# Centering of adapter 1's tiles: from VectorE to ScalarE, with a product on GpSimd

## The reference, cut to what matters

```python
h = gelu(einsum('bsh,bhk->bsk', x, W_down[role]) + b_down[role])
y = x + einsum('bsk,bkh->bsh', h, W_up[role]) + b_up[role]
mean, var = y.mean(-1), y.var(-1)
out = (y - mean) * rsqrt(var + 1e-5) * gamma[role] + beta[role]
```

## Time and profile before

| | us |
|---|---|
| median of 3 runs | 196.28 (194.84 to 196.86) |
| profiled execution, its own time | 194.28 |
| its span, first to last instruction | 192.5 |
| TensorE, VectorE, ScalarE, GpSimd busy | 183.5, 114.7, 81.1, 42.1 |

### The profile page before, as it was taken

How to read it: one execution, slowest core, us unless ns; L and a number is a source line. 1 busy time by engine, 2 the same in 40 slices (tenths; PEclk the granted TensorE clock), 3 DMA queues, 4 the chain that set the end, 5 groups by cost and what they waited for, 6 DMA issues and landing times.

```text
span 192.5 us, 3157 instructions
## 1 busy us (share of the span) xinstructions
PE 183.5 (95%) x1031; PEld 158.0 (82%) x1031; DVE 114.7 (60%) x283; ACT 81.1 (42%) x164; POOL 42.1 (22%) x72
## 2 busy tenths in 40 slices
PE   7989999999999999999999999999999999999980
PEld 7857887979888888888888888888888989999850
DVE  2987998799658898450392622041442146558983
ACT  0643774643798206970144543003545333221340
POOL 8475667100000006000230000000110013226431
PEclk9999999999999999999999999999999999999998
DMA  3778589994301172000000070000100004432122
GB/s 103 237 218 278 166 263 262 275 306 152 109 3 60 51 239 88 0 3 0 0 0 3 0 218 0 0 0 5 55 0 0 3 0 116 125 118 78 33 61 77
DMA packets 18874, 17.83 MB, mean 93 GB/s; under 512 B 2145, under 2 KB 17322, under 8 KB 18858
## 3 DMA queue, kind: packets, MB, share of 16 engines
q1 hardware_dynamic: 17008, 14.79, 24.8%
q0 software_dynamic: 928, 2.11, 4.1%
q10 hardware_dynamic: 922, 0.73, 1.2%
HBM read 16.58 MB, written 1.05 MB: 92 GB/s over the span
## 4 chain that ended last, share of the span: by engine, by line
PE 82%; DVE 8%; DMA 4%; issue 2%; POOL 1%; ACT 0%; ACTq 0%; DVEq 0%
PE bank L640 21%; PE bank L641 20%; PE bank L642 20%; PE bank L752 5%; PE bank L768 5%; DMA stage<-in_L_cond_Wq 2%; PE bank L745 2%; PE bank L821 2%; DMA x_tok<-in_x,from_row_i 2%; PE bank L808 2%; PE bank L778 1%; DVE yA L1331 1%; PE bank L747 1%; DVE yB L1350 1%; DVE yB L1357 1%
## 5 line engine op out<-in xcount | busy, mean ns | idle before, releaser
L1412 DVE TENSOR_TENSOR g_l<-g_full,g_h 128x512 fp32r<-128x512 f32 x32 | 22.1, 692 | 38.9 <-ACT g_h L1037 38.8
L1034 ACT ACTIVATE g_full<-bank,vecs 128x512 f32<-128x512 f32 x32 | 22.1, 691 | 40.8 <-PE bank L642 39.8
L1524 POOL TENSOR_TENSOR mvA<-mvA,power 128x1 f32<-128x1 f32 x16 | 9.4, 588 | 70.2 <-DVE mvA L1267 70.1
L1037 ACT ACTIVATE g_h<-bank,vecs 128x512 fp32r<-128x512 f32 x32 | 21.9, 684 | 0.0
L1551 POOL TENSOR_TENSOR x1T<-x1T,cms_full 128x512 f32<-128x512 f32 x4 | 6.0, 1498 | 56.4 <-DVE cms_full L1427 56.4
L640 PE MATMUL bank<-g_h,mw_h 128*128 128x256 f32 (+1 forms) x48 | 16.0, 334 | 0.0
L642 PE MATMUL bank<-g_h,mw_l 128*128 128x256 f32 (+1 forms) x48 | 15.3, 318 | 0.0
L641 PE MATMUL bank<-g_l,mw_h 128*128 128x256 f32 (+1 forms) x48 | 15.3, 318 | 0.0
L640 PE MATMUL bank<-ao_h,mw_h 128*128 128x512 f32 x32 | 13.1, 411 | 0.0
L640 PE MATMUL bank<-ao_h,cw_h 128*128 128x512 f32 x32 | 12.5, 392 | 0.0
L642 PE MATMUL bank<-ao_h,mw_l 128*128 128x512 f32 x32 | 12.5, 391 | 0.0
(11 more groups left out here) (265 smaller groups left out, 441.8 us busy)
## 6 DMA issues: line engine op xcount, KB each, us to landing
stage<-in_L_cond_mW SPq DMA_DIRECT2D x6, 512.0 KB, 3.2
stage<-in_L_cond_cW SPq DMA_DIRECT2D x4, 512.0 KB, 6.7
wdA<-in_L_cond_W_down SPq DMA_DIRECT2D x14, 128.0 KB, 3.3
wuA<-in_L_cond_W_up SPq DMA_DIRECT2D x14, 128.0 KB, 3.3
wdB<-in_L_cond_W_down SPq DMA_DIRECT2D x12, 128.0 KB, 3.1
wuB<-in_L_cond_W_up SPq DMA_DIRECT2D x12, 128.0 KB, 3.0
wd_last<-in_L_cond_W_down SPq DMA_DIRECT2D x4, 128.0 KB, 2.2
wu_last<-in_L_cond_W_up SPq DMA_DIRECT2D x4, 128.0 KB, 2.1
```

The lines of the kernel that those rows point to most:

```text
L1034: act.activation(g_full[n % 2][:, 0:width], bank[b][:, 0:width], ACT.Gelu, bias=bias)
L1037: act.activation(g[0][:, j, 0:width], bank[b][:, 0:width], ACT.Gelu, bias=bias).then_inc(g_high, 1)
L1412: dve.tensor_tensor(g[1][:, j, 0:width], g_full[n % 2][:, 0:width], g[0][:, j, 0:width].bitcast(F32), ALU.subtract).then_inc(g_ready, 1)
L1524: pool.tensor_tensor(mv[:, k, 2:3], mv[:, k, 1:2], power[:, :], ALU.pow).then_inc(done, 1)
```

## The change

VectorE's centering of adapter 1 is left out. ScalarE gets a step center: it waits for rstdA_ready and computes Identity(scale * y + bias) in one activation, with the power (mvA column 2) as scale and column 3 as bias. GpSimd writes that column, -mean * power, in a tensor_scalar behind the power; link makes it wait for the power through GpSimd's own semaphore, and rstdA_ready is now raised by the product. ScalarE's new step stands where center stands in the list. Adapter 2's centering stays as it was.

```diff
--- before.py
+++ after.py
@@ -270,7 +270,7 @@
         hB = [place(f"hB{i}", [P, 2, P], F32) for i in range(XSLOTS)]
         yB = [place(f"yB{i}", [P, D], F32) for i in range(YSLOTS)]
         statsA = place("statsA", [P, YSLOTS, 9], F32)
-        mvA = place("mvA", [P, YSLOTS, 3], F32)
+        mvA = place("mvA", [P, YSLOTS, 4], F32)
         statsB = place("statsB", [P, YSLOTS, 9], F32)
         mvB = place("mvB", [P, YSLOTS, 3], F32)
         table = {}
@@ -953,6 +953,18 @@
                                          ACT.Gelu, bias=seq_vecs[:, BD[kind], n:n + 1])
                 ins.then_inc(raw, 1)
 
+            def center(layer, c):
+
+                if layer:
+                    return
+                i = lane_a(layer, c)
+                k = i % YSLOTS
+                act.wait_ge(rstdA_ready, i + 1)
+                if i >= YSLOTS:
+                    act.wait_ge(normA_T_ps, i - YSLOTS + 1)
+                act.activation(yA[k][:, :], bank[chain_bank(layer, c)][:, 0:D], ACT.Identity,
+                               bias=mvA[:, k, 3:4], scale=mvA[:, k, 2:3]).then_inc(normA_ready, 1)
+
             def turn0(c):
 
                 if c in MESSY:
@@ -1046,7 +1058,7 @@
                         act.copy(cms[phase][0][:, m, :], cms_full[:, m, :]).then_inc(cms_high, 1)
 
             do = {"vectors": vectors, "chunk_vecs": chunk_vectors, "spread": spread_ids, "seq_vecs": seq_vectors, "fold_transpose": fold_transpose, "fold": fold,
-                  "load": load, "down": down, "turn": lambda layer, c: (turn2 if layer else turn0)(c), "values": values, "finish": finish,
+                  "load": load, "down": down, "center": center, "turn": lambda layer, c: (turn2 if layer else turn0)(c), "values": values, "finish": finish,
                   "project": project, "scores": scores, "mix": mix,
                   "hidden": hidden, "outer": outer}
             for name, *args in steps:
@@ -1323,6 +1335,8 @@
                     moments(y, statsA, mvA, k, varA_ready)
 
             def center(layer, c):
+                if layer == 0:
+                    return
                 i = lane_a(layer, c)
                 k = i % YSLOTS
                 dve.wait_ge(rstdA_ready, i + 1)
@@ -1528,7 +1542,14 @@
                     rstd(mvB, c % YSLOTS, varB_ready, c + 1, rstdB_ready)
                 else:
                     i = lane_a(layer, c)
-                    rstd(mvA, i % YSLOTS, varA_ready, i + 1, rstdA_ready)
+                    k = i % YSLOTS
+                    if layer:
+                        rstd(mvA, k, varA_ready, i + 1, rstdA_ready)
+                        return
+                    pool.wait_ge(varA_ready, i + 1)
+                    link(pool.tensor_tensor(mvA[:, k, 2:3], mvA[:, k, 1:2], power[:, :], ALU.pow))
+                    pool.tensor_scalar(mvA[:, k, 3:4], mvA[:, k, 0:1], mvA[:, k, 2:3], -1.0,
+                                       ALU.mult, ALU.mult).then_inc(rstdA_ready, 1)
 
             def finish(layer, c):
```

## The result

The changed kernel takes 199.25 us (median of 6 runs, 198.25 to 201.07); the kernel before, in the same six rounds, takes 194.82 (194.55 to 196.86). The ratio is 1.024 (95% interval 1.020 to 1.028): slower, by some 4.7 us (4.4 by the medians). The forecast was 199.3 with 197.2 to 200.9. The absolute time came out, but partly by luck: three more runs brought the median of before down from 196.28 to 194.82, and the forecast said +3.0. The profiled executions differ by more still: 194.28 and 199.37 us, spans 192.5 and 197.6, where the steps gave 197.3. So the direction and the place were right, and 1.4 to 2.1 us are to be found.

What follows compares the result with a forecast made beforehand. TensorE was taken to bound the kernel, so delays of the attention's mix reach the end. Steps through GpSimd's and ScalarE's queues made it 3.1 us late; less 0.1, +3.0 on 196.28 gives 199.3 us, range 197.2 to 200.9.

Steps and rivals of the forecast that it cites:

- What bounds: First adapter, 16 to 42 us: TensorE has at most 0.93 us idle to win; delays of the mix go through.
- ScalarE's centering: Identity with scale and bias for each adapter 1 tile on ScalarE: 0.56 us, 0.46 in a packed queue.
- GpSimd's product: Product behind each adapter 1 power on GpSimd: 0.40 us a tile with the wait, ends 0.16 and 0.71.
- Step 1: GpSimd at the head: gather of window 4 some 0.5 us late, third centering on ScalarE 23.5 to 24.06.
- Step 2: ScalarE's queue behind the third centering: TensorE's up of window 6 1.7 us late, turn of window 3 1.6.
- Step 3: GpSimd in the middle: token-table gathers end at 34.8, 2.1 us late, as are window 4's turn and the scores.
- Step 4: Exp table load behind window 5's centering on ScalarE: copies and mix 3.1 us late, 0.95 beyond the scores.
- The clock: Granted clock falling in this stage's stalls: listed as a sign the forecast was wrong, with no size given.
- Only the table load: Rival: earlier steps give nothing, the load behind the last centering costs +1.5, 197.8 us; chance 0.20.
- The relief of VectorE: Rival: TensorE's down at 23.46 moves forward, gain up to 0.93 us, 195.4 us; chance 0.06.
- The dearer switch of tables: Rival: the table load holds ScalarE longer after other work, by +1.4, to 200.7 us; chance 0.04.
- The sum: Whole kernel: +3.1 less 0.1 for VectorE's earlier start on the rest order, +3.0 on 196.28, giving 199.3 us.

Runs made afterwards that it cites:

- e10: Kernel before, VectorE centering window 2 after window 3's moments and before the late biases, GpSimd's clear of probs_T behind window 2's power: 194.74 us, ratio 1.000.
- e11: Kernel before, VectorE centering windows 2 and 3 after window 3's moments, ahead of late biases and first weights piece: 195.43 us, ratio 1.003.
- e8: Changed kernel with the low part of the first half's x1 zeroed by a VectorE memset instead of a two-input subtraction: 199.74 us, one run, not read as time.
- e3: Changed kernel with the four token-table gathers moved behind the centering of window 5: 197.93 us, ratio 1.016.
- e7: e6 with ScalarE's centerings of windows 2 and 3 further back in its queue: 197.74 us, ratio 1.016.
- e12: e2 with ScalarE's order of e7 (centerings of windows 2 and 3 further back): 195.96 us, ratio 1.006.
- e5: Changed kernel with 8 unread matmuls ahead of TensorE's turn of window 4: 199.00 us, ratio 1.022.
- e2: Changed kernel without GpSimd's product; ScalarE centers with the plain mean as bias: 196.43 us, ratio 1.008.
- e9: e7 with the Exp table load back behind the centering of window 5: 197.41 us, ratio 1.012.
- e6: e3 with the Exp table load ahead of ScalarE's centering of window 4: 198.91 us, ratio 1.020.
- e4: Changed kernel with 16 unread matmuls ahead of TensorE's turn of window 4: 200.11 us, ratio 1.026.

## Why the prediction was right, and where it was off

- *What bounds.* Right: the stage had under 1 us to win, and a delay of the mix goes to the end nearly whole (mix +5.35, span +5.1). Of the wait at 23.46 only 0.2 us could be won, and e10 and e11 turned none of it into time.
- *ScalarE's centering.* 0.56 us estimated, 557 to 589 ns measured.
- *GpSimd's product.* 0.40 estimated, 0.35 where nothing disturbs it. The term failed not in its size but in being one number: two products took 0.48 and 1.14 us, and two powers 1.04 and 1.02. The prediction had the rule of the Trainium skill for it ("SBUF — State Buffer", "SBUF: two separate sides": an exclusive lock between GpSimd and a VectorE operation with two SBUF inputs), and let it move nothing but the upper end. e8 bears the rule out: 1.14 against 0.27 us.
- *Step 1.* The third centering ended at 24.73, from the first Gelu 9.09; predicted 24.06, which is 8.81. Close; most of the 0.28 is the product of 0.48 us. Missed: that the gather of window 4 had no slack. Its step was followed to the next power in GpSimd's queue, but not to TensorE's transposes, which came at 22.24 before and waited until 23.45 for the landing. It cost nothing by itself, although the chain names it: TensorE waited for the third centering behind it all the same. In e3 there was no such wait at the transposes (22.72), the one for the centering was 0.95 us instead of 0.46, and the up of window 6 came 11.4 us after the first Gelu, against 11.2 here.
- *Step 2.* The up of window 6 was 2.4 us late (2.0 from the first Gelu), predicted 1.7; the turn of window 3 was 2.2 late (1.8), predicted 1.6. Mechanism shown by e7 and e12, and the miss is the 0.28 us by which the third centering was late in step 1.
- *Step 3.* This is the step that failed in size. The gathers were to end at 34.8 and ended at 36.68, from the first Gelu 1.5 us later than forecast. The powers of windows 6 and 7 began 0.6 later than the step had them: 0.3 from step 2, and 0.3 because VectorE took up the moments of window 6 only 0.1 us sooner after TensorE than before, and not 0.4. Powers and products of the two windows took 1.2 us more than the step had, by the power of 1.02 and the product of 1.14 of window 7. The gathers themselves ran 0.3 shorter. The turn of window 4 was to be 2.1 us late and was 4.15 (3.8 from the first Gelu).
- *Step 4.* As the term that decides it failed: the table load was hidden behind the scores, since step 3 had grown past it, and in place of it stood GpSimd's queue and then the clock, which made the scores 0.9 us longer (2.83 us of records against 1.95 in e5). As a mechanism it is right, and it waits right behind: in e5, at the full clock, the scores end at 41.28 and the small activation behind the load at 41.32; the load binds in e2, e3, e9 and e12, and in e6 and e7 it holds the turn.
- *The clock.* The text named its fall as a way to be wrong and gave it no price. Its own signs had TensorE idle for over 1.5 us ahead of the mix, so the case could have had a term of its own. In the profiled execution it came behind the wait at the turn instead, and cost 1.2 us up to the mix (7.20 us from the turn against 6.00 in e5), 0.9 of them in the scores.
- *The rivals.* "Only the table load" was to cost +1.5; e12, where the product is gone, ScalarE's queue is in the new order and the load is left, costs +1.1 (with 0.37 us of wait at the turn besides). It holds for that kernel, not for the change. The relief of VectorE won nothing. The dearer switch of tables is ruled out once more: the small activation ran 0.02 us behind the load (39.13 + 1.28, 40.43), so the drain that the Trainium skill counts ("ScalarE: Activation LUTs", "What ACT_TABLE_LOAD costs") does not show here either.
- *The sum.* +3.0 against +4.7 in the timed runs and +5.1 in the profiled ones. The mix's 5.35 us split into 0.39 of the first gather, 3.76 up to the turn of window 4 (2.1 forecast, the rest being step 3's 1.5 and roundings), and 1.20 from there on, of the clock, where 0.95 of the table load was forecast. The time of 199.3 came out because the median of before that it was added to lay 1.5 us too high.

## What to carry to other kernels

An operation that moves to another engine takes its waits with it: before moving it, read what stands behind it in the new queue (here a Gelu, a copy and a table load), and what stands behind the small helper that it needs on a third one (here the gathers and powers of the next windows and four table gathers). An engine that is busy half of the time is not free if it works in order; ScalarE had 14 of 26 us of work and still held TensorE. And if a wait of some 2 us on TensorE is part of a forecast, name what a fall of the clock behind it would cost (1.2 us here) as a bound: it came in one profiled execution and stayed out in others.

## What the runs showed of the hardware

- GpSimd's 128x1 tensor_scalar takes 0.26 us and its power of that size 0.55; beside VectorE's two-input operation on 128x1024 the former took 1.14 us, up to 1.51 in e7, ending 0.38 us behind that operation in both, and 0.27 with a memset in that place.
- After a wait of 1.99 us at the turn of window 4 the granted clock fell to 0.50 for some 3 us of scores and values; after waits of 1.87 (e6, e7) and 1.59 (e8) at the same place it stayed at 1.00, and with 8 or 16 matmuls in the wait (e5, e4) as well. The wait alone does not settle it: at the transposes near 14.4 us the clock fell behind a wait of 0.85 us in e8 and stayed at 1.00 behind 1.03 us in the changed kernel. Each is one profiled execution.
- The table load of 1.28 us ran in ScalarE's order in every run here, behind a centering or ahead of one; with the centerings in that queue its place was a choice between two waits (1.01 us at the mix in e3, 1.87 us at the turn in e6).
